# TensorE's signals in the edge stream of a two-layer graph network: two steps a block, each closed by a drain

## What is computed

```
h        = relu(concat(x[src], edge_attr) @ W1.T + b1)
agg      = segment_sum(h @ W2.T + b2, dst)
x1       = layernorm(x + GRU(agg, x))
agg2[i]  = sum over edges with src = i of x1[dst]
x2       = layernorm(x1 + (agg2 / max(deg, 1)) @ weight + x1 @ root + bias)
```

## Time and profile before

| | |
|---|---|
| three runs | 5907.3, 5913.37, 5916.59 us |
| profiled execution, its own time | 5894.56 us |
| span of its instructions | 5892.9 us |
| mean granted TensorE clock | 0.837 of full |
| busy share PE / PEld / DVE / ACT / POOL | 75 / 64 / 56 / 40 / 54% |
| mean busy share of the 16 DMA engines in the stream | 0.60 |

### The profile page before, as it was taken

How to read it: one execution, slowest core, us unless ns; L and a number is a source line. 1 busy time by engine, 2 the same in 40 slices (tenths; PEclk the granted TensorE clock), 3 DMA queues, 4 the chain that set the end, 5 groups by cost and what they waited for, 6 DMA issues and landing times.

```text
span 5892.9 us, 89839 instructions
## 1 busy us (share of the span) xinstructions
PE 4424.1 (75%) x30332; PEld 3765.1 (64%) x30332; DVE 3327.6 (56%) x9964; ACT 2357.5 (40%) x4278; POOL 3209.3 (54%) x3198
## 2 busy tenths in 40 slices
PE   6577777777777777777777777777777777777776
PEld 5465666666666666666666666667666666666664
DVE  4444656565656555555656565656565656555555
ACT  2244343434343434344444434343434343434343
POOL 2566555655565555555555656555655555555510
PEclk8667989798978888888888888879797989888889
DMA  6444747575656566565656575647575656566556
GB/s 192 91 127 137 197 141 207 150 200 149 190 162 184 168 174 174 166 184 158 187 156 194 151 201 151 197 141 206 149 202 150 194 158 186 163 179 171 169 146 176
DMA packets 1017762, 998.71 MB, mean 169 GB/s; under 512 B 204167, under 2 KB 857548, under 8 KB 1016921
## 3 DMA queue, kind: packets, MB, share of 16 engines
q1 hardware_dynamic: 830878, 459.88, 28.2%
q10 hardware_dynamic: 84075, 321.56, 17.1%
q0 software_dynamic: 102352, 211.43, 14.6%
HBM read 655.22 MB, written 337.22 MB: 168 GB/s over the span
## 4 chain that ended last, share of the span: by engine, by line
PE 50%; another core or an unknown queue 16%; DVE 15%; issue 10%; ACT 6%; DMA 1%; DVEq 1%; POOL 0%; SPq 0%; ACTq 0%; POOLq 0%
PE stream_pse L1199 12%; PE stream_psa L1208 10%; PE stream_psw L1223 9%; PE stream_pse L1191 6%; PE stream_psw_third L1223 5%; DVE stream_col L969 4%; ACT stream_a_sb L884 4%; DVE stream_sums L979 3%; DVE stream_sums L983 2%; ACT stream_hid L846 1%; DVE ring L947 1%; PE stream_psw L1247 1%; DVE stream_acc L939 1%; DVE stream_row L964 1%
## 5 line engine op out<-in xcount | busy, mean ns | idle before, releaser
L829 POOL DMA_INDIRECT ring<-y,ring x3105 | 3137.7, 1011 | 2314.9 <-ACT stream_hid L846 1492.4
L884 ACT CAST stream_a_sb<-stream_psa 98x512 f16<-98x512 f32 x3125 | 1768.8, 585 | 2909.1 <-PE stream_psa L1208 1125.5
L947 DVE TENSOR_TENSOR ring<-stream_pse,ring 128x384 f32<-128x384 f32 x1250 | 612.2, 490 | 1862.9 <-remote 836.8
L1208 PE MATMUL stream_psa<-stream_col,stream_row 128*98 128x256 f16 x6250 | 1291.4, 311 | 477.6 <-ACT stream_a_sb L884 289.0
L1223 PE MATMUL stream_psw<-stream_z,stream_strip 128*128 128x257 f16 x5850 | 936.4, 293 | 382.4 <-DVE stream_sums L983 333.1
L1208 PEld LDWEIGHTS stream_psa<-stream_col,stream_row 128*98 128x98 f16 x6250 | 823.9, 143 | 623.6 <-issue 392.2
L1199 PE MATMUL stream_pse<-w1b,ring 128*128 128x128 f32 x6250 | 1154.8, 325 | 49.8 <-issue 23.8
L1199 PEld LDWEIGHTS stream_pse<-w1b,ring 128*128 128x128 f32 x6250 | 997.7, 231 | 101.2 <-issue 61.1
L969 DVE TENSOR_TENSOR stream_col<-iota_lo,stream_twin 128x1536 f16<-128x1536 f16 x1250 | 1022.2, 818 | 0.0
L1223 PEld LDWEIGHTS stream_psw<-stream_z,stream_strip 128*128 128x128 f16 x5850 | 594.0, 105 | 542.1 <-issue 306.2
L1191 PEld LDWEIGHTS stream_pse<-stream_seg,stream_hid 128*128 128x128 f32 x6250 | 836.2, 211 | 1.1
(11 more groups left out here) (203 smaller groups left out, 2063.8 us busy)
## 6 DMA issues: line engine op xcount, KB each, us to landing
A<-stream_a_sb ACTq DMA_DIRECT2D x625, 490.0 KB
stream_strip<-A SPq DMA_DIRECT2D x1862, 160.0 KB
ring<-in_ea_blocks_dram SPq DMA_DIRECT2D x625, 160.0 KB
ring<-y,ring POOLq DMA_INDIRECT x3125
stream_col<-A SPq DMA_DIRECT2D x84, 96.0 KB, 2.5
prologue_xt<-in_xT_dram SPq DMA_DIRECT2D x14, 448.0 KB
y<-prologue_ysb SPq DMA_DIRECT2D x14, 448.0 KB
ring<-r SPq DMA_DIRECT2D x49, 128.0 KB, 2.5
```

The source lines that it names most:

```text
L829: nc.gpsimd.indirect_dma_start(out=yg[s.c % 4][:, t, :], out_offset=None, in_=h.y, in_offset=bass.IndirectOffsetOnAxis(ap=idx[s.c // (PH / ...
L884: nc.scalar.copy(a_sb[s.c % AR][0:RW, j, :], psa[BANK[j]][0:RW, :]).then_inc(a_out, 1)
L947: V.tensor_tensor(yg[s.c % 4][:, lo:hi, :], pse[half][:, 0:(hi - lo) * D].rearrange("p (t d) -> p t d", d=D), yg[s.c % 4][:, lo:hi, :], AL ...
L1208: last = nc.tensor.matmul(psa[BANK[j]][0:RW, e * LOS:(e + 1) * LOS], row1[s.c % 2][:, 2 * j + e, :], col1[s.c % 2][:, 2 * j + e, :], start ...
```

## The change

Edge product, counts and units lose their increments. TensorE gets two drains a block, each of which raises `step_done` by one: one after counts 2 (ahead of the segment), one at the block's end (ahead of the gate work). Everything that waited for `e_done`, `a_done` or `unit_done` in the stream now waits for `step_done`: the first half of the products, counts 0 to 2 and the first two units for the first drain, the rest for the second. Count banks turn by the running number of the pair modulo 3, and a pair waits for the copy three before it. VectorE's adds of units are split: those of the first two units stand in the first part of its block, those of the others behind `add_segment`. SyncE's and ScalarE's waits for units go by `unit_added`, or by a `unit_done` that counts the last stage alone.

```diff
@@ SyncE
-                reach(sp, e_done, s.times(2, -2))
+                reach(sp, step_done, s.times(2, -2))
...
-                            sp.wait_ge(unit_done, ph.n(TS, 2 * (c - RING) + 3))
+                            sp.wait_ge(unit_added, ph.n(TS, 2 * (c - RING) + 3))
@@ ScalarE
-                    act.wait_ge(a_done, s.times(PAIRS, j + 1))
-                    nc.scalar.copy(a_sb[s.c % AR][0:RW, j, :], psa[BANK[j]][0:RW, :]).then_inc(a_out, 1)
+                    act.wait_ge(step_done, s.times(2, 1 if j < FRONT else 2))
+                    nc.scalar.copy(a_sb[s.c % AR][0:RW, j, :], psa[s.times(PAIRS, j) % 3][0:RW, :]).then_inc(a_out, 1)
@@ VectorE
-                dve.wait_ge(e_done, s.times(2, 4 if s.c < BLOCKS - 1 else 3))
+                dve.wait_ge(step_done, s.times(2, 4 if s.c < BLOCKS - 1 else 3))
...
-                dve.wait_ge(e_done, s.times(2, half + 1))
+                dve.wait_ge(step_done, s.times(2, half + 1))
...
-            def unit_first(ph, u):
-                dve.wait_ge(unit_done, ph.n(TS, u + 2))
+            def unit_first(s, ph, n, u):
+                dve.wait_ge(step_done, s.times(2, 1 if n < 2 else 2))
...
-                order = []
-                for n, u in enumerate(units):
-                    order.append((unit_first, u))
-                    if n:
-                        order.append((unit_second, units[n - 1]))
-                if units:
-                    order.append((unit_second, units[-1]))
+                work = list(enumerate(units))
+                front = [(unit_first, w) for w in work[:2]] + [(unit_second, w) for w in work[:2]]
+                back = []
+                for w in work[2:]:
+                    back.append((unit_first, w))
+                    if w[0] > 2:
+                        back.append((unit_second, work[w[0] - 1]))
+                if work[2:]:
+                    back.append((unit_second, work[-1]))
...
                 segment_hot(s)
-                adds(1)
+                adds(front, 1)
                 if more:
                     rows(nxt)
-                adds(2)
+                adds(front, 2)
                 if more:
                     cols(nxt, 0)
+                adds(front, 1)
                 add_gathered(s, 1)
                 if s.c >= 1:
                     add_segment(s.back(1), seg_at[x])
-                adds(3)
+                adds(back, 3)
                 if more:
                     cols(nxt, 1)
-                adds(99)
+                adds(back, 99)
@@ TensorE
-                last.then_inc(e_done, 1)
...
-                reach(pe, a_out, s.times(PAIRS, SPENT[j]))
+                reach(pe, a_out, s.times(PAIRS, j - 2))
...
-                last.then_inc(a_done, 1)
...
-                last.then_inc(unit_done, 1)
...
                 counts(s, 2)
+                pe.drain().then_inc(step_done, 1)
                 if s.c >= 1:
                     segment(s.back(1))
                 edge_product(s, 1)
...
                 next_unit()
+                pe.drain().then_inc(step_done, 1)
                 if k is not None:
                     gate_work(k, ph)
```

More of the change, by code:

```diff
@@ L645, in strips_of @@
     return [u // 2 for u in units_of(k) if u % 2 == 0]
+FRONT = 3
 def uses(x, n):
@@ L701, in stream @@
         idx_in, ea_in, a_stored = h.idx_in, h.ea_in, m.sems("a_stored", AR)
-        e_done, sum_done, relu_done = m.sem("e_done"), m.sem("sum_done"), m.sem("relu_done")
+        step_done, sum_done, relu_done = m.sem("step_done"), m.sem("sum_done"), m.sem("relu_done")
         seg1_ready, agg_done = m.sem("seg1_ready"), m.sem("agg_done")
-        twin_ready, hot_ready, a_done, a_out = m.sem("twin_ready"), m.sem("hot_ready"), m.sem("a_done"), m.sem("a_out")
+        twin_ready, hot_ready, a_out = m.sem("twin_ready"), m.sem("hot_ready"), m.sem("a_out")
         ea_ready, cleared, rolled = m.sem("ea_ready"), m.sem("cleared"), m.sem("rolled")
@@ L763, in body @@
                 if k == 10 and ph.p == ITER:
-                    sp.wait_ge(unit_done, ITER * TS + 1)
+                    sp.wait_ge(unit_added, ITER * TS + 1)
                     for c in range(RING - 1):
@@ L769, in body @@
                         if c >= RING:
[L770 removed]
+                            sp.wait_ge(unit_added, ph.n(TS, 2 * (c - RING) + 3))
                         elif c == 0:
[L772 removed]
+                            sp.wait_ge(unit_added, ph.n(TS, 1))
                         load_strip(ph, c, strip[c % RING], strip_in[c % RING])
@@ L807, in _ @@
                     if c >= 1:
-                        sp.wait_ge(unit_done, ITER * TS + 1 + 2 * c)
+                        sp.wait_ge(unit_done, 2 * c)
                     load_strip(LAST[0], c + RING - 1, strip[(c - 1) % RING], strip_in[(c - 1) % RING])
@@ L869, in gate_work @@
                     if not ph.col:
-                        act.wait_ge(unit_done, ph.n(TS, 1))
+                        act.wait_ge(unit_added, ph.n(TS, 1))
                     nc.scalar.activation(zz[:, 0:T, 0:D], xb[:, 0:T], ACT.Copy, scale=SCALE).then_inc(hi_ready, 1)
@@ L962, in rows @@
                 dve.wait_ge(twin_ready, s.times(1, 1))
-                reach(dve, a_done, s.times(PAIRS, -PAIRS))
+                reach(dve, step_done, s.times(2, -2))
                 V.tensor_tensor(row1[s.c % 2][:].rearrange("p g (a b) -> p g a b", b=2), paired(RW, GB),
@@ L1052, in body, with adds @@
                 units = units_of(k) if k is not None and ph.p < ITER else []
-                ops = [(f, u) for u in units for f in (unit_first, unit_second)]
-                order = []
-                for n, u in enumerate(units):
-                    order.append((unit_first, u))
-                    if n:
-                        order.append((unit_second, units[n - 1]))
-                if units:
-                    order.append((unit_second, units[-1]))
-                def adds(n):
+                work = list(enumerate(units))
[7 more added lines that the diff above has]
+                    back.append((unit_second, work[-1]))
+                def adds(order, n):
                     for _ in range(n):
                         if order:
-                            f, u = order.pop(0)
-                            f(ph, u)
+                            f, (turn, u) = order.pop(0)
+                            f(s, ph, turn, u)
                 if k == 0:
@@ L1119, in add_high @@
             def add_high(c):
-                dve.wait_ge(unit_done, ITER * TS + 2 * c + 3)
+                dve.wait_ge(unit_done, 2 * c + 2)
                 V.tensor_tensor(sums[:, 2 * c:2 * c + 2, :], sums[:, 2 * c:2 * c + 2, :], pair[c % 2][:, :, 0:P + 1], ALU.add
@@ L1205, in counts @@
                     pe.wait_ge(hot_ready, s.times(2, 1 if j == 0 else 2))
-                reach(pe, a_out, s.times(PAIRS, SPENT[j]))
+                reach(pe, a_out, s.times(PAIRS, j - 2))
                 for e in range(2):
-                    last = nc.tensor.matmul(psa[BANK[j]][0:RW, e * LOS:(e + 1) * LOS], row1[s.c % 2][:, 2 * j + e, :],
+                    last = nc.tensor.matmul(psa[s.times(PAIRS, j) % 3][0:RW, e * LOS:(e + 1) * LOS], row1[s.c % 2][:, 2 * j + e, :],
                                             col1[s.c % 2][:, 2 * j + e, :], start=True, stop=True)
-                last.then_inc(a_done, 1)
+                return last
             def unit(ph, u):
@@ L1267, in next_unit @@
                     if units:
-                        unit(ph, units.pop(0))
+                        return unit(ph, units.pop(0))
                 pe.wait_ge(ea_in[s.c % 2], s.turn(2, 16))
@@ L1301, in _ @@
             node_part(0)
-            segment(Step(0, BLOCKS - 1)).then_inc(e_done, 1)
+            segment(Step(0, BLOCKS - 1)).then_inc(step_done, 1)
             pe.wait_ge(xq_ready, LAST[1].n(1, 1))
```

6 lines of the change are left out of this document (2 added, 4 removed).

## The result

The changed kernel takes 6115.09 us in the median of four runs (6087.3 to 6134.2), beside 5914.98 us for the kernel before on the same chip: ratio 1.0335, interval [1.0291, 1.0379]. The forecast was 5577 us; the measured time lies above the range (6000) and on the other side. The profiled execution took 6122.75 us, with a granted clock of 0.848.

The account below looks back on a forecast made before the run. The prediction took a loop of waits to bound the kernel, with TensorE's signals late during GpSimd's gathers. Signals -754, drains +256 and units' adds +162 made -336 us, a median of 5577 us (-5.7%), range 5187 to 6000.

Parts of the forecast that it names:

- The reading of what holds: TensorE's matmul signals queue while GpSimd issues gathers and come out when these end; 16.1% of the stream's chain, 879 us.
- it closes into a loop: Late second half product delays VectorE's add, the add the relu, the relu GpSimd's next gathers, which again hold signals.
- The step that failed: Signals term: two instead of twelve a block can't queue; 0.1 us each stays, 125 of 879 us, so -754.
- 0.35 us for pair 2: Lateness of count pair 2's signal in one block, taken as upper end of what each remaining signal waits.
- The rival "the drain is held too": TensorE's completion itself is late, so each drain stands 0.67 us, 838 us in all; 6290 us, chance 0.22.
- the threshold of 0.37: Hold in us a drain from which the rival of held drains decides the outcome.
- units' adds: Units 2 to 4 added only after the block's end: TensorE waits 0.45 us in 360 blocks, +162 us.
- Drains: 0.26 us each: Lost overlap 0.16 and weight load 0.105 us at each of TensorE's two drains a block; +256 us together.
- Signals counted: Aside: ten fewer increments in each of 625 blocks at 0.026 us would give 163 us.
- Copies at nothing: Three copies starting together after the first drain cost 0, covered by segment and edge product or the gather's pace.
- SyncE's later loads: Edge attributes issued some 2.4 us later on paper, hidden by the 8.8 us block in between: 0.
- The stages: Sign of being right: some 8.2 us a block with units, 8 without; wrong if units blocks take 9 or more.

Follow-up runs that it names:

- e9: Kernel before, on a late chip, with one plain ScalarE transfer of consecutive rows a block in place of GpSimd's five gathers: 4399.42 us, 0.7444.
- e3: Kernel before, on a prompt chip, with one plain ScalarE transfer of consecutive rows a block in place of GpSimd's five gathers: 4385.76 us, 0.9586.
- e7: Changed kernel without its drains, the last matmul of each step raising the signal, on a late chip: 6012.37 us, 1.0179 to the kernel before.
- e1: Changed kernel without its drains, the last matmul of each step raising the signal, on a prompt chip: 4833.33 us, 1.0568 to the kernel before.
- e14: Kernel before, on a prompt chip, GpSimd's fourth gather of a block also waiting for the second half product three blocks before: 4575.57 us, 0.9992.
- e16: The changed kernel, unaltered, on a prompt chip: 5169.14 us, 1.1273 to the kernel before.
- e2: Kernel before, all its signals kept, plus two drains a block that raise nothing, on a prompt chip: 4975.47 us, 1.0873.
- e8: Kernel before, all its signals kept, plus two drains a block that raise nothing, on a late chip: 6297.63 us, 1.066.
- e10: The changed kernel, unaltered, on a late chip: 6101.12 us, 1.0328 to the kernel before.
- e11: Kernel before, on a prompt chip, GpSimd issuing plain transfers of 128 consecutive rows instead of indirect ones: 4379.86 us, 0.9545.
- e12 to e15: Kernel before (1.0003, 0.9992) and changed kernel (1.1275 twice) on prompt chips, GpSimd's fourth gather of a block waiting for work three blocks before.

## Why the prediction was wrong

**The reading of what holds was right, as far as it went.** Signals of TensorE's matmuls come late, and it goes with the gathers. That it closes into a loop over add, relu and next train is argued from the waits; no run on a late chip broke the loop alone. e9 takes the gathers away: -1511 us on a late chip, beside -187 us on a prompt one (e3), where nothing is held. The hold is thus worth some 1320 us, more than the 879 us that I read from the chain, so a part of its price stood in the chain under other names. That a queue forms was part of the reading, too; that part is the step that failed.

**The step that failed: "I take it that a queue can no longer form with two signals a block, and that each of the 1250 still waits 0.1 us."** The number of signals is not what makes them late. In e7 two signals a block have as large an unknown share (18%) as twelve, the mean lateness of a signal is the same (1.05 and 1.08 us), and one that has none ahead of it comes 1.66 us late. The bound that I took from the earlier trace rows, 0.35 us for pair 2, was one short delay taken for a ceiling; the mean over both steps' ends in the same rows, 0.94 us, stood in the rival. In the change the two signals sit on drains, and there 0.66 us is measured for each of 1250, 827 us against 125: the term was -754 and should have been about -52 (-879 + 827). With the other two terms as forecast the sum would be 5892.9 - 52 + 256 + 162 = 6259 us of span, beside 6121.0 measured.

**The rival "the drain is held too" is what happened**, in mechanism and price: 0.67 us a drain forecast, 0.66 measured, the threshold of 0.37 passed, TensorE standing for "issue" ahead of the first matmul behind a drain. That the price is so near is partly luck, as it came from two signals of one block. Its 6290 us were 175 too many. The one term that is clearly too high is **units' adds**: forecast +162, and TensorE's wait ahead of units fell instead, from 382.4 + 224.1 to 11.9 + 9.6 us. When TensorE stands behind a drain, VectorE catches up with the adds meanwhile. The wait that was forecast exists where signals are prompt and no drain stands: 96.0 + 46.4 us for adds ahead of units in e1, beside 15.2 + 7.1 in e14 (another prompt chip, early adds) and 0.2 in e16, where the drains cover it. On a late chip it doesn't show: e7 has 375.3 + 141.7 us, the kernel before 333.1 + 209.3.

**Drains: 0.26 us each** were too few. Of these, 0.105 us was for starting again; from the release to the next matmul it takes 0.37 us in the mean on a late chip and 0.40 on a prompt one. In time, e2 gives 402/1250 = 0.32 us each, with the signals unchanged and nothing held. e8, on a late chip, gives 388/1250 = 0.31, but there the drains are held as well, so that this is a balance of what they cost and what they spare. With 827 us held, 0.32 us a drain and nothing for the adds the sum would be 5892.9 - 879 + 827 + 402 = 6243 us, still 122 above the measured span. So the terms don't simply add up, and where the 122 lie is not shown.

**Signals counted.** The aside with 26 ns an increment took ten fewer signals in each of 625 blocks. Only 324 blocks have ten fewer, 36 have nine and 265 have five: 4889 signals and 127 us by the same figure, in place of 163. The forecast's sum did not use it.

**Copies at nothing** held: TensorE's wait for copies at counts fell from 289.0 to 19.9 us. SyncE's later loads cost nothing that shows: TensorE waits 3.6 us for edge attributes at L1204.

**The stages**: 8.2 us with units and 8 without were forecast, "9 us or more" was named as what would prove it wrong; 9.06 and 7.99 (opening), 9.38 (gate work) came.

**What stood against the rival.** The chance that I gave it, 0.22, was held down by TensorE's usual spacing in a train of matmuls. That spacing says when matmuls start, not when the last one counts as complete. The change beside the same signals on matmuls is at 1.0328 beside 1.0179 on a late chip (e10, e7), and at 1.1273 beside 1.0568 on prompt ones (e16, e1, in two groups). The Trainium skill, PSUM — Partial Sum Buffer, section on engine and sequencer instructions, puts the increment on the matmul, as a matter of correctness and without a price, and says that a drain waits for the engine to go fully idle; the runs agree in that TensorE stands until the drain's release. The Trainium skill, SBUF — State Buffer, section on who interferes with whom, says that TensorE waits on nobody. That fits the prompt chips, with 21 ns at a drain; on late chips its completion, though perhaps not its work, comes late while GpSimd gathers and not without the gathers (e9), and there the measurement decides.

## What to carry to other kernels

Put the increment on the matmul that makes the result, one for each consumer; a drain as a carrier of signals costs 0.3 us even where nothing else is wrong (e2), and when completions are late it moves the lateness from the consumers onto the producer. Before you count a held time as won, ask what is held: if it is the completion, fewer signals don't shorten it, and everything that waits for completion (a drain above all) takes it over. What could have told ahead of the change is the lateness of each single signal over the whole stream: 1.08 us in the mean for the edge product's, three times the 0.35 us of one pair.

## What the runs showed of the hardware that was not expected

The same program on different chips took 5910 to 5920 us on two and 4573 to 4592 on three, 29% apart, while each repeats itself within some tenths of a per cent. GpSimd's own time for a gather is nearly the same on both (for kernels that gather alike, 1.01 us in the kernel before and 1.02 in e14), and with plain transfers in place of the gathers both take nearly the same (4399 and 4386 us). TensorE's granted clock differs (0.84 and 0.90), but it does not mark the chip: without the gathers it is 0.923 on both (e9, e3). Lateness in a trace can thus belong to the chip, or to what else differs between two sessions, and not to the program. The change is slower on both, but nearly four times as much on the prompt kind (12.7% and 3.3%).

Open: why the chips differ; whether it is the indirect form, any transfer that GpSimd issues, or the scattered rows which holds completions; and whether breaking up the train of gathers helps on a late chip. The runs for the last two (e11, e12 to e15) are on prompt chips. One hint is in the trace of the change: of the 412 held end drains, 366 have no new gather within 1.5 us. In these the release comes 1.02 us (median) after the last gather's end on GpSimd, while the last packet of the gathers ends another 0.61 us after the release. So in these the hold does not wait for the gathered rows to have landed. No version that was run with its gathers beat the kernel before.
